# Shared experts of a two-layer MoE kernel: weights held on TensorE, the tokens' turned rows moving through

## The chip, the cores and the metric

The kernel runs on one core of a Trainium2 chip. The metric is the device time of one execution in microseconds. A core has TensorE (matmuls; PE in the views, PEld for its weight loads), VectorE (DVE), ScalarE (ACT), GpSimd (POOL) and SyncE (SP, here the issuer of most DMAs). They run their own instruction lists and wait for one another by semaphores.

## The reference, cut to what matters

Two layers over x of 8 x 256 tokens, D = 256. Each layer normalises x, computes an attention s and a mixture of experts g from the normalised rows, and adds s * silu(g) to x. The part that is changed is the shared expert of each layer, an MLP with 352 hidden columns that every token goes through:

```python
sg = silu(jnp.einsum('bsd,fd->bsf', x, Wsg))           # layer 0, FS = 352
su = jnp.einsum('bsd,fd->bsf', x, Wsu)
shared_out = jnp.einsum('bsf,df->bsd', sg * su, Wsd)
...
z = jax.nn.silu(xf @ Sg.T) * (xf @ Su.T) @ Sd.T        # layer 1, ISH = 352
```

Beside it each token goes through 2 of 8 routed experts in layer 0 and 4 of 16 in layer 1, with 176 hidden columns each. All is float32.

## The kernel before

The span begins with layer 0's attention (to about 362 us), then come layer 0's expert blocks, layer 1's attention (about 550 to 1580 us), and layer 1's expert blocks to the end. The expert part of a layer is one list of units, each of 128 rows. First come the routed units (NB0 = 39, NB1 = 79): rows gathered by expert are read from DRAM, put through that expert, and stored to DRAM (yg). Then come sixteen shared units, one for each tile of 128 tokens. I call these sixteen the shared stage of a layer, and count their tiles by c, with n = NB + c.

A shared unit goes through these helpers, which stand with the same names in pe_blocks0, act_blocks0, dve_blocks0 and in their twins for layer 1 (lines in brackets: layer 0, layer 1):

- turn_x on TensorE (L938, L1944): two transposes put the tile's rows on their side; copy_x on ScalarE (L1079, L2029) copies them to SBUF as xbT. In layer 0, from some tile on, a second pair of transposes (L942) and a small product (L950) make the logits of layer 1's router.
- shared_gate_up on TensorE (L987, L1980): xbT is the loaded (stationary) operand, the weights of gate and up move through it, 352 columns at a time: 2 projections x 2 halves of D = 4 matmuls. Gate goes to PSUM bank 2, up to bank 3, in every unit. A float32 matmul shows as two records in the trace.
- tanh on ScalarE (L1085, L2035), then the two steps of hidden on VectorE (L1147 and L1151, L2084 and L2088): silu(gate) * up, tokens on the partitions.
- turn_h on TensorE (L968, L1961): three transposes put h on its side into bank 4 or 5; copy_h on ScalarE (L1097, L2047) brings it to SBUF (the routed units copy theirs on VectorE).
- shared_down on TensorE (L996, L1989): three matmuls of 256 moving columns, to bank 6 or 7.
- combine on VectorE (L1166 and L1169; L2101 and L2106): adds the routed results of the tile's tokens, which GpSimd gathers from yg by an indirect DMA for each expert of a token, two a tile in layer 0 (L1271), four in layer 1 (L2147). Buffers for two tiles exist: the gathers for tile c start once combine(c-2) is done. The first of them waits until all routed results are stored.
- out_tanh (L1103, L2053), gate_out (L1175; L2114 and L2116), and add_out (L1180, L2121), which adds to x_res. In layer 0 the product with S, the attention's result, is made by GpSimd (mix, L1254), and VectorE then takes the statistics for layer 1's normalisation (L1188, L1190), with which GpSimd makes the reciprocal root (norm_pow, L1259 and L1261).

The order on each engine is written out by hand. TensorE, for each tile: shared_gate_up(n), logits, turn_x(n+1), shared_down(n-1) (for c = 0 the last routed unit's down instead, L976 and L978, L1969 and L1971), turn_h(n). VectorE: hidden(n), gate_out(c-2), combine(c-1), then scale, add_out and statistics of earlier tiles. GpSimd in layer 0: norm_pow(c-4), the two gathers of c, mix(c-3); in layer 1 the gathers alone. As gate and up have one pair of banks, shared_gate_up(n) waits until hidden(n-1) has read them (`pe.wait_ge(h_ready, n)`).

L1446, L1447 and L1448 are matmuls of layer 1's attention with 128 loaded and 128 (or 64) moving float32 columns.

Of the kernel before, what the change touches and what calls it, by code (L numbers as in the profile page):

```python
# [26 lines left out]
P = 128  # L27
# [82 lines left out]
def build(nc, A, out, phases=3):  # L110
    with ExitStack() as ctx:
# [177 lines left out]
        th_b = carve("blocks", 2, FS0)  # L289
# [629 lines left out]
        def pe_blocks0(pe):  # L919
# [93 lines left out]
            for c in range(TILES):  # L1013
# [9 lines left out]
                turn_h(n, FS_CHUNKS)  # L1023
# [47 lines left out]
        def act_blocks0(act):  # L1071
# [40 lines left out]
            for c in range(TILES):  # L1112
                n = NB0 + c
                tanh(n, FS0)
# [6 lines left out]
                copy_h(n)  # L1121
# [16 lines left out]
        def dve_blocks0(dve):  # L1138
            def hidden(n, width):
                routed = n < NB0  # L1140
                gate = ps[:, 2 + n % 2, 0:F0] if routed else ps[:, 2, 0:FS0]
                up = ps[:, 2 + n % 2, F0:2 * F0] if routed else ps[:, 3, 0:FS0]
                th = th_b[:, n % 2, 0:width]
# [3 lines left out]
                dve.scalar_tensor_tensor(th, th, 1.0, gate, ALU.add, ALU.mult).then_inc(half_step, 1)  # L1147
# [3 lines left out]
                dve.tensor_tensor(h_pad[:, n % 2, 0:width], th, up, ALU.mult).then_inc(h_ready, 1)  # L1151
# [51 lines left out]
            for b in range(NB0):  # L1203
                hidden(b, F0)
# [3 lines left out]
            for c in range(TILES):  # L1208
                hidden(NB0 + c, FS0)
# [710 lines left out]
        def again(sem, done):  # L1920
# [3 lines left out]
        gu4_done, th4_ready, half4_step, h4_ready, h4_turned, h4T_copied, y4_done, y4_copied = (  # L1924
            again(n, UNITS) for n in (gu_done, th_ready, half_step, h_ready, h_turned, hT_copied, y_done, y_copied))
# [7 lines left out]
        def pe_blocks1(pe):  # L1933
# [40 lines left out]
            def shared_gate_up(n):  # L1974
                pe.wait_ge(x4_copied.sem, x4_copied.at(0, n + 1))
                pe.wait_ge(h4_ready.sem, h4_ready.at(0, n))
                for which in range(2):
                    for kc in range(KC):
                        at = (2 * kc + which) * FS1
                        last = pe.matmul(ps[:, 2 + which, 0:FS1], xb4T[:, n % 2, kc * P:(kc + 1) * P], shared1[:, at:at + FS1],  # L1980
                                         start=kc == 0, stop=kc == KC - 1)
                last.then_inc(gu4_done.sem, 1)

            def shared_down(n):
                pe.wait_ge(h4T_copied.sem, h4T_copied.at(0, n + 1))
                pe.wait_ge(y4_copied.sem, y4_copied.at(0, n - 1))
                for f in range(FS_CHUNKS):
                    at = 2 * KC * FS1 + f * D
                    last = pe.matmul(ps[:, 6 + n % 2, 0:D], h4T[:, n % 2, f * P:(f + 1) * P], shared1[:, at:at + D],  # L1989
# [22 lines left out]
            for c in range(TILES):  # L2012
# [8 lines left out]
                turn_h(n, FS_CHUNKS)  # L2021
            shared_down(UNITS1 - 1)

        def act_blocks1(act):
# [6 lines left out]
            def tanh(n, width):  # L2031
                act.wait_ge(gu4_done.sem, gu4_done.at(0, n + 1))
                if n >= 2:
                    act.wait_ge(h4_ready.sem, h4_ready.at(0, n - 1))
                act.activation(th4[:, n % 2, 0:width], ps[:, 2 + (n % 2 if n < NB1 else 0), 0:width], ACT.Tanh, scale=0.5)\  # L2035
                   .then_inc(th4_ready.sem, 1)
# [6 lines left out]

            def copy_h(n):
                act.wait_ge(h4_turned.sem, h4_turned.at(0, n + 1))
                act.wait_ge(y4_done.sem, y4_done.at(0, n - 1))
                act.copy(h4T[:, n % 2, :], ps[:, 4 + n % 2, 0:HCOLS]).then_inc(h4T_copied.sem, 1)  # L2047
# [14 lines left out]
            for c in range(TILES):  # L2062
                n = NB1 + c
                tanh(n, FS1)
# [6 lines left out]
                copy_h(n)  # L2071
# [3 lines left out]
        def dve_blocks1(dve):  # L2075
            def hidden(n, width):
                routed = n < NB1
                gate = ps[:, 2 + n % 2, 0:F1] if routed else ps[:, 2, 0:FS1]
                up = ps[:, 2 + n % 2, F1:2 * F1] if routed else ps[:, 3, 0:FS1]
                th = th4[:, n % 2, 0:width]  # L2080
# [524 lines left out]
```

## Time and profile before

| | us |
|---|---|
| median of 3 runs | 1880.08 |
| lowest and highest | 1878.42, 1880.09 |
| the profiled execution's own time | 1896.83 |
| its span | 1895.0 |
| TensorE busy (PE) | 1768.4 (93%) |
| VectorE busy | 1265.7 (67%) |
| ScalarE busy | 908.8 (48%) |
| GpSimd busy | 857.2 (45%) |
| granted TensorE clock, mean over the span | 0.975 of full speed |

The span runs from the first to the last instruction of the profiled execution. A busy share is taken over the whole span, attention included; the two shared stages, from about 459 to 554 us and from about 1782 us to the end, are a tenth of it. In the views, "issue" after an arrow is time in which the engine waited for nothing that the profile shows, and "remote" a releaser that the profile doesn't know.

### The profile page before, as it was taken

To read this page: it belongs to the slowest core of one execution; us is meant where nothing else is said; L and a number is where in the kernel's file an instruction comes from. 1 tells how busy PE (TensorE), PEld (TensorE's weight loads), DVE (VectorE), ACT (ScalarE), POOL (GpSimd) and SP (SyncE) were. 2 spreads that over 40 slices of the span, in tenths; PEclk is the share of its full clock that TensorE was granted. 3 is DMA by queue.
4 is the path that set the end of the run, shared out by engine and by line. 5 is a ranking of instruction groups with operands and counts; after the bars stand their busy time and mean duration, and the time that the engine had idled before them with its cause. 6 is when DMAs were issued, how large, how long until landed. Compare 5 with 4: busy or idle time off the path is not lost.

```text
span 1895.0 us, 34165 instructions
## 1 busy us (share of the span) xinstructions
PE 1768.4 (93%) x11310; PEld 1401.9 (74%) x11310; DVE 1265.7 (67%) x2787; ACT 908.8 (48%) x2986; POOL 857.2 (45%) x943
## 2 busy tenths in 40 slices
PE   6999988899879999999999999999999997999976
PEld 4666666677658887888888888888888885777653
DVE  4888988643676888886767666666666663444465
ACT  3777767543334444444544544445445443444321
POOL 2011024100665655657767667677676661000264
PEclk8999999999989999999999999999999998999998
DMA  7965543244220000000000000000001223333333
GB/s 238 304 217 164 187 140 112 92 129 142 99 85 1 1 12 1 6 1 15 21 16 15 20 16 20 16 12 23 13 12 45 85 102 123 107 106 107 100 118 108
DMA packets 104692, 148.39 MB, mean 78 GB/s; under 512 B 11888, under 2 KB 84720, under 8 KB 102096
## 3 DMA queue, kind: packets, MB, share of 16 engines
q1 hardware_dynamic: 95168, 119.95, 19.6%
q0 software_dynamic: 9216, 25.18, 4.0%
q8 instruction: 107, 1.75, 0.4%
q10 hardware_dynamic: 144, 1.05, 0.1%
q14 instruction: 57, 0.47, 0.1%
HBM read 81.64 MB, written 64.49 MB: 77 GB/s over the span
## 4 chain that ended last, share of the span: by engine, by line
PE 78%; DVE 10%; issue 4%; POOL 3%; ACT 2%; another core or an unknown queue 1%; DMA 1%; SPq 0%; DVEq 0%; ACTq 0%; POOLq 0%
PE ps L1419 12%; PE ps L1434 9%; PE ps L1506 5%; PE ps L1952 5%; PE ps L1460 5%; PE ps L705 4%; PE ps L1448 3%; PE ps L1447 3%; PE ps L1446 3%; PE ps L959 2%; PE ps L1441 2%; PE ps L1969 2%; PE ps L1971 2%; PE ps L724 2%; PE ps L695 2%
## 5 line engine op out<-in xcount | busy, mean ns | idle before, releaser
L1419 PE MATMUL ps<-work,weights 128*128 128x256 f32 x1024 | 248.6, 386 | 1.2 <-DVE work L1692 1.1
L1434 PE MATMUL ps<-split 128*128 128x512 f32 x768 | 227.8, 419 | 0.0
L1419 PEld LDWEIGHTS ps<-work,weights 128*128 128x128 f32 x1024 | 186.3, 191 | 23.8 <-DVE work L1692 1.4
L1834 POOL TENSOR_TENSOR work<-work,rope 128x512 f32<-128x512 f32 x128 | 164.8, 1288 | 54.0 <-ACT work L1607 54.0
L2147 POOL DMA_INDIRECT work<-yg,work x64 | 62.7, 980 | 238.7 <-DMA yg<-work 207.3
L1840 POOL TENSOR_TENSOR work<-work 128x512 f32<-128x512 f32 x128 | 164.5, 1285 | 5.0
L1434 PEld LDWEIGHTS ps<-split 128*128 128x128 f32 x768 | 130.7, 190 | 24.8
L827 DVE COPY work<-ps 128x384 f32<-128x384 f32 x256 | 130.0, 549 | 19.8 <-PE ps L705 19.5
L810 ACT ACTIVATE work<-ps,work 128x128 f32<-128x128 f32 x256 | 94.5, 369 | 84.5 <-DVE work L907 74.5
L705 PE MATMUL ps<-ident,work 128*128 128x128 f32 x768 | 115.4, 282 | 17.3 <-DVE work L827 15.4
L1506 PE MATMUL ps<-weights,work 128*128 128x256 f32 x512 | 124.1, 386 | 2.5 <-ACT work L1663 2.5
L513 POOL DMA_INDIRECT xg<-work x96 | 97.2, 1013 | 62.5 <-PE ps L695 39.8
L2084 DVE SCALAR_TENSOR_TENSOR work<-work,ps 128x176 f32<-128x176 f32 (+1 forms) x95 | 35.0, 369 | 133.8 <-ACT work L2035 123.5
L1714 DVE TENSOR_TENSOR work<-ps,keep_w 128x384 f32<-128x384 f32 x128 | 65.4, 553 | 87.2 <-PE ps L1442 86.8
L812 ACT ACTIVATE work<-ps,work 128x256 f32<-128x256 f32 x256 | 121.6, 475 | 0.0
L705 PEld LDWEIGHTS ps<-ident,work 128*128 128x128 f32 x768 | 88.6, 144 | 41.7 <-ACT work L812 19.1
L1460 PE MATMUL ps<-work 64*128 64x256 f32 (+1 forms) x1024 | 106.1, 349 | 13.7 <-issue 10.9
L1648 ACT ACTIVATE work<-ps,work 128x128 f32<-128x128 f32 x256 | 90.6, 366 | 51.4 <-PE ps L1448 51.1
L1727 DVE RECIPROCAL work<-ps 128x256 f32<-128x256 f32 x64 | 111.9, 1748 | 0.0
L1506 PEld LDWEIGHTS ps<-weights,work 128*128 128x128 f32 x512 | 99.3, 194 | 17.0 <-ACT work L1663 3.1
L1613 ACT COPY work<-ps 128x256 f32<-128x256 f32 x128 | 47.2, 368 | 130.3 <-PE ps L1434 130.3
L1460 PEld LDWEIGHTS ps<-work 64*128 64x128 f32 x1024 | 86.9, 195 | 30.2 <-issue 14.1
(240 smaller groups left out, 4447.3 us busy)
## 6 DMA issues: line engine op xcount, KB each, us to landing
heads_by_part<-split SPq DMA_DIRECT2D x64, 256.0 KB, 4.1
split<-heads_by_part SPq DMA_DIRECT2D x64, 256.0 KB
work<-xg SPq DMA_DIRECT2D x118, 128.0 KB
yg<-work SPq DMA_DIRECT2D x118, 128.0 KB, 1.7
xg<-work SPq DMA_DIRECT2D x13, 1024.0 KB, 5.9
weights<-in_w SPq DMA_DIRECT2D x8, 1024.0 KB, 6.1
weights<-in_f SPq DMA_DIRECT2D x8, 1024.0 KB, 5.0
weights<-in_f SPq DMA_DIRECT2D x8, 608.0 KB, 4.4
```

The costliest lines, as they stand in the source:

```text
L513: pool.indirect_dma_start(out=rows, out_offset=bass.IndirectOffsetOnAxis(ap=self.index[:, k, c:c + 1], axis=0), in_=src, in_offset=None).t ...
L705: last = pe.transpose(ps[:, 4 + hh, k * P:(k + 1) * P], prob[:, g % RING, hh, k * P:(k + 1) * P], ident[:, :])
L812: act.activation(pr[:, P:BLK], sc[:, 0:SEQ], ACT.Exp, bias=nmax[:, g % RING, 1, hh:hh + 1], accum_out=total[:, bb, 1, h:h + 1]).then_inc(e ...
L827: dve.tensor_copy(probT[:, g % RINGT, hh, :], ps[:, 4 + hh, 0:BLK]).then_inc(probT_ready.sem, 1)
L1419: last = pe.matmul(ps[:, 2, which * SEQ:(which + 1) * SEQ], w1(h, (which * KC + kc) * P, P), xT[:, kc, :], start=kc == 0, stop=kc == KC - 1)
L1434: last = pe.matmul(ps[:, 3, :], x1_split[:, xp, kc, c * P:(c + 1) * P], w_vg[:, n % 2, wp, kc, :], start=i == 0, stop=i == KC * len(TERMS) ...
L1460: last = pe.matmul(ps[:, 4 + hh, at], k[rows, half, keys], q[rows, half, queries], start=half == 0, stop=half == 1)
L1506: last = pe.matmul(ps[:, 7, c * D:(c + 1) * D], ogT[:, hh, c * P:(c + 1) * P], weights[:, W1O + h * D:W1O + (h + 1) * D], start=h == 0 and ...
L1727: dve.reciprocal(enz[:, n % 2, :, :].rearrange("p c n -> p (c n)"), ps[:, 0, SEQ:2 * SEQ])\
L1834: pool.tensor_tensor(qk[:, h % 4, :, :], raw[:, h % 2, :, :], rope[:, 0, :].unsqueeze(1).broadcast_to([P, 2, SEQ]), ALU.mult).then_inc(rot ...
L1840: pool.tensor_tensor(qk[:, h % 4, :, :], qk[:, h % 4, :, :], rot_s[:, h % 2, :, :], ALU.add)\
L1952: last = pe.matmul(ps[:, 2 + b % 2, 0:GUW], xb4T[:, b % 2, kc * P:(kc + 1) * P], experts1[:, bass.ds(offset[b] + kc * GUW, GUW)], start=kc ...
```

## The change

The operands of the gate and up projections change places. The weights are the loaded operand, in chunks of 128, 128 and 96 of the 352 hidden columns, and xbT, 128 tokens wide, moves through. That makes 12 matmuls of 128 moving columns in place of 4 of 352. Gate and up come out with the hidden columns on the partitions, three chunks side by side in 384 columns, which is the shape that shared_down loads. So turn_h and copy_h go for shared units, and hidden's second step writes hbT itself. Gate and up get two pairs of banks, 2 and 3, 4 and 5, in turn, and shared_gate_up(n) waits for hidden of unit n-2. The last chunk's down product reads 96 rows. tanh and hidden work on 384 columns (the last chunk's rows 96 to 127 are whatever lies in the bank, and nothing reads them). The order of the rest stays.

```diff
             def shared_gate_up(n):
+
+                bank = 2 + 2 * ((n - NB0) % 2)
                 pe.wait_ge(x_copied, n + 1)
-                pe.wait_ge(h_ready, n)
+                pe.wait_ge(h_ready, max(n - 1, NB0))
+                if n == NB0 + 1:
+                    pe.wait_ge(hT_copied, NB0)
                 for which in range(2):
-                    for kc in range(KC):
-                        at = (2 * kc + which) * FS0
-                        last = pe.matmul(ps[:, 2 + which, 0:FS0], xbT[:, n % 2, kc * P:(kc + 1) * P], shared0[:, at:at + FS0],
-                                         start=kc == 0, stop=kc == KC - 1)
+                    for f in range(FS_CHUNKS):
+                        width = min(P, FS0 - f * P)
+                        for kc in range(KC):
+                            at = (2 * kc + which) * FS0 + f * P
+                            last = pe.matmul(ps[0:width, bank + which, f * P:(f + 1) * P], shared0[:, at:at + width],
+                                             xbT[:, n % 2, kc * P:(kc + 1) * P], start=kc == 0, stop=kc == KC - 1)
                 last.then_inc(gu_done, 1)
 
             def shared_down(n):
-                pe.wait_ge(hT_copied, n + 1)
+                pe.wait_ge(h_ready, n + 1)
                 pe.wait_ge(y_copied, n - 1)
                 for f in range(FS_CHUNKS):
                     at = 2 * KC * FS0 + f * D
-                    last = pe.matmul(ps[:, 6 + n % 2, 0:D], hbT[:, n % 2, f * P:(f + 1) * P], shared0[:, at:at + D],
+                    rows = min(P, FS0 - f * P)
+                    last = pe.matmul(ps[:, 6 + n % 2, 0:D], hbT[0:rows, n % 2, f * P:(f + 1) * P], shared0[0:rows, at:at + D],
                                      start=f == 0, stop=f == FS_CHUNKS - 1)
...
                     shared_down(n - 1)
-                turn_h(n, FS_CHUNKS)
...
             def tanh(n, width):
+                bank = 2 + n % 2 if n < NB0 else 2 + 2 * ((n - NB0) % 2)
                 act.wait_ge(gu_done, n + 1)
                 if n >= 2:
                     act.wait_ge(h_ready, n - 1)
-                act.activation(th_b[:, n % 2, 0:width], ps[:, 2 + (n % 2 if n < NB0 else 0), 0:width], ACT.Tanh, scale=0.5)\
-                   .then_inc(th_ready, 1)
+                act.activation(th_b[:, n % 2, 0:width], ps[:, bank, 0:width], ACT.Tanh, scale=0.5).then_inc(th_ready, 1)
...
-            def copy_h(n):
-                act.wait_ge(h_turned, n + 1)
-                act.wait_ge(y_done, n - 1)
-                act.copy(hbT[:, n % 2, :], ps[:, 4 + n % 2, 0:HCOLS]).then_inc(hT_copied, 1)
...
-                tanh(n, FS0)
+                tanh(n, HCOLS)
                 if c + 1 < TILES:
                     copy_x(n + 1)
                 if c == 0:
                     copy_y(NB0 - 1)
                 if c >= 2:
                     out_tanh(c - 2)
-                copy_h(n)
...
+            def shared_hidden(n):
+                bank, th = 2 + 2 * ((n - NB0) % 2), th_b[:, n % 2, :]
+                dve.wait_ge(th_ready, n + 1)
+                dve.scalar_tensor_tensor(th, th, 1.0, ps[:, bank, 0:HCOLS], ALU.add, ALU.mult).then_inc(half_step, 1)
+                dve.wait_ge(half_step, n + 1)
+                dve.wait_ge(y_done, n - 1)
+                dve.tensor_tensor(hbT[:, n % 2, :], th, ps[:, bank + 1, 0:HCOLS], ALU.mult).then_inc(h_ready, 1)
...
-                hidden(NB0 + c, FS0)
+                shared_hidden(NB0 + c)
...
-        h4 = carve("experts", 2, HCOLS)
+        h4 = carve("experts", 2, 2 * P)
         h4T = carve("experts", 2, HCOLS)
-        th4 = carve("experts", 2, FS1)
+        th4 = carve("experts", 2, HCOLS)
```

Layer 1 gets the same edits under its own names (h4_ready, h4T and so on). The semaphores h4_turned and h4T_copied start from NB0, where they started from NB0 + 16, as the shared units no longer count on them.

## Rows read from the trace of the kernel before

**Rows 1.** Busy by stretches: PE, PEld, DVE, ACT, POOL; clock, DMA share, GB/s.

```profile
522.01:527.38 5.37, 5.06 (x26) 3.71 (x26) 3.60 (x11) 1.86 (x5) 3.56 (x6) 1.00 0.17 50
...
1863.31:1867.89 4.58, 4.58 (x20) 2.94 (x20) 3.98 (x10) 1.57 (x4) 3.64 (x4) 1.00 0.58 171
...
1787.90:1882.00 94.10, 71.98 (x276) 47.32 (x274) 55.52 (x124) 21.82 (x57) 62.71 (x64) 0.92 0.41 121
```

**Rows 2.** The chain that ended last, layer 0: start us, us, what.

```profile
459.65 2.37 PE ps L987 x8
...
462.68 0.45 PE ps L978 x2
...
463.54 1.71 DMA yg<-work
...
467.36 6.49 DMA work<-yg,work
...
541.64 0.55 PE ps L968 x3
```

**Rows 3.** Timeline, layer 0, one period: start us, us, instruction, idle before.

```profile
522.01 0.19 POOL L1259 TENSOR_TENSOR work<-work,minus_half 128x1 f32<-128x1 f32 x1 [1.22 <-DVE work L1190]
...
526.19 0.43 DVE L1180 SCALAR_TENSOR_TENSOR x_res<-work,x_res 128x256 f32<-128x256 f32 x1 [1.63 <-POOL work L1254]
...
527.38 0.19 POOL L1259 TENSOR_TENSOR work<-work,minus_half 128x1 f32<-128x1 f32 x1 [1.22 <-DVE work L1190]
```

**Rows 4.** Who waited for whom, in 484:540 and 1787:1895 (total, times, longest).

```profile
DVE x_res L1180 <- POOL work L1254: 17.5, 10, 2.7
...
POOL work L2147 <- DVE work L2106: 12.8, 4, 4.7
```

**Rows 5.** The chain that ended last, a tile of layer 1.

```profile
1861.13 0.47 ACT work L2035
...
1861.63 0.53 DVE work L2084
...
1862.76 0.55 PE ps L1961 x3
1863.31 2.37 PE ps L1980 x8
1865.68 0.40 PE ps L1944 x2
1866.08 1.30 PE ps L1989 x6
1867.38 0.51 PE ps L1961 x3
```

**Rows 6.** Timeline, layer 1: gathers on GpSimd, VectorE's combine.

```profile
1787.90 0.99 POOL L2147 DMA_INDIRECT work<-yg,work  x1 [207.33 <-DMA yg<-work]
...
1794.22 0.95 POOL L2147 DMA_INDIRECT work<-yg,work  x1 [0.31 <-issue]
...
1794.54 0.48 DVE L2101 SCALAR_TENSOR_TENSOR work<-work,ps 128x256 f32<-128x256 f32 x1 [3.93 <-DMA work<-yg,work]
...
1887.90 0.48 DVE L2101 SCALAR_TENSOR_TENSOR work<-work,ps 128x256 f32<-128x256 f32 x1 [1.17 <-PE ps L1989]
```

**Rows 7.** ScalarE in 1782:1890 (busy, mean ns, idle before), and one tanh.

```profile
L2047 ACT COPY work<-ps 128x384 f32<-128x384 f32 x16 | 7.7, 479 | 34.9 <-remote 17.0 <-PE ps L1961 12.8 <-issue 5.1
L2035 ACT ACTIVATE work<-ps 128x352 f32<-128x352 f32 x16 | 7.4, 465 | 36.9 <-PE ps L1980 18.0 <-remote 15.2 <-issue 3.8
...
1804.20 0.47 ACT L2035 ACTIVATE work<-ps 128x352 f32<-128x352 f32 x1 [5.52 <-remote]
```

**Rows 8.** 128 by 128 matmuls of attention, their loads (ns, min/median/max).

```profile
1311.32 0.39 PE L1446 MATMUL ps<-work 128*128 128x128 f32 x2
...
1312.43 0.39 PE L1448 MATMUL ps<-work 128*128 128x128 f32 x2
...
L1448 PEld LDWEIGHTS ps<-work x512: 192/192/192, 576.5 to 1573.7; 128*128 128x128 f32 x171
```

More of the change, by code:

```diff
@@ L1138, in dve_blocks0, with hidden @@
         def dve_blocks0(dve):
[L1139 to L1143, printed above, removed]
+            def hidden(n):
+                th = th_b[:, n % 2, 0:F0]
                 if n == 0:
@@ L1203, in dve_blocks0 @@
             for b in range(NB0):
-                hidden(b, F0)
+                hidden(b)
                 if b >= 1:
@@ L1923, in build @@
         x4_turned, x4_copied = again(x_turned, UNITS + BEHIND), again(x_copied, UNITS + BEHIND)
-        gu4_done, th4_ready, half4_step, h4_ready, h4_turned, h4T_copied, y4_done, y4_copied = (
-            again(n, UNITS) for n in (gu_done, th_ready, half_step, h_ready, h_turned, hT_copied, y_done, y_copied))
+        gu4_done, th4_ready, half4_step, h4_ready, y4_done, y4_copied = (
+            again(n, UNITS) for n in (gu_done, th_ready, half_step, h_ready, y_done, y_copied))
+        h4_turned, h4T_copied = again(h_turned, NB0), again(hT_copied, NB0)
         x4_loaded = [again(xb_loaded[n], 16 * len(range(n, NB0, RINGX))) for n in range(RINGX)]
@@ L1974, in shared_gate_up @@
             def shared_gate_up(n):
+                bank = 2 + 2 * ((n - NB1) % 2)
                 pe.wait_ge(x4_copied.sem, x4_copied.at(0, n + 1))
-                pe.wait_ge(h4_ready.sem, h4_ready.at(0, n))
+                pe.wait_ge(h4_ready.sem, h4_ready.at(0, max(n - 1, NB1)))
+                if n == NB1 + 1:
+                    pe.wait_ge(h4T_copied.sem, h4T_copied.at(0, NB1))
                 for which in range(2):
[L1978 to L1981, printed above, removed]
+                    for f in range(FS_CHUNKS):
+                        width = min(P, FS1 - f * P)
+                        for kc in range(KC):
+                            at = (2 * kc + which) * FS1 + f * P
+                            last = pe.matmul(ps[0:width, bank + which, f * P:(f + 1) * P], shared1[:, at:at + width],
+                                             xb4T[:, n % 2, kc * P:(kc + 1) * P], start=kc == 0, stop=kc == KC - 1)
                 last.then_inc(gu4_done.sem, 1)
             def shared_down(n):
-                pe.wait_ge(h4T_copied.sem, h4T_copied.at(0, n + 1))
+                pe.wait_ge(h4_ready.sem, h4_ready.at(0, n + 1))
                 pe.wait_ge(y4_copied.sem, y4_copied.at(0, n - 1))
@@ L1988, in shared_down @@
                     at = 2 * KC * FS1 + f * D
-                    last = pe.matmul(ps[:, 6 + n % 2, 0:D], h4T[:, n % 2, f * P:(f + 1) * P], shared1[:, at:at + D],
+                    rows = min(P, FS1 - f * P)
+                    last = pe.matmul(ps[:, 6 + n % 2, 0:D], h4T[0:rows, n % 2, f * P:(f + 1) * P], shared1[0:rows, at:at + D],
                                      start=f == 0, stop=f == FS_CHUNKS - 1)
@@ L2063, in act_blocks1 @@
                 n = NB1 + c
-                tanh(n, FS1)
+                tanh(n, HCOLS)
                 if c + 1 < TILES:
@@ L2075, in dve_blocks1, with hidden @@
         def dve_blocks1(dve):
[L2076 to L2080, printed above, removed]
+            def hidden(n):
+                th = th4[:, n % 2, 0:F1]
                 if n == 0:
@@ L2087, in hidden, with shared_hidden @@
                     dve.wait_ge(h4_turned.sem, h4_turned.at(0, n - 1))
-                dve.tensor_tensor(h4[:, n % 2, 0:width], th, up, ALU.mult).then_inc(h4_ready.sem, 1)
+                dve.tensor_tensor(h4[:, n % 2, 0:F1], th, ps[:, 2 + n % 2, F1:2 * F1], ALU.mult).then_inc(h4_ready.sem, 1)
+            def shared_hidden(n):
+                bank, th = 2 + 2 * ((n - NB1) % 2), th4[:, n % 2, :]
+                dve.wait_ge(th4_ready.sem, th4_ready.at(0, n + 1))
+                dve.scalar_tensor_tensor(th, th, 1.0, ps[:, bank, 0:HCOLS], ALU.add, ALU.mult).then_inc(half4_step.sem, 1)
+                dve.wait_ge(half4_step.sem, half4_step.at(0, n + 1))
+                dve.wait_ge(y4_done.sem, y4_done.at(0, n - 1))
+                dve.tensor_tensor(h4T[:, n % 2, :], th, ps[:, bank + 1, 0:HCOLS], ALU.mult).then_inc(h4_ready.sem, 1)
             def copy_h(b):
@@ L2124, in dve_blocks1 @@
             for b in range(NB1):
-                hidden(b, F1)
+                hidden(b)
                 if b >= 1:
@@ L2129, in dve_blocks1 @@
             for c in range(TILES):
-                hidden(NB1 + c, FS1)
+                shared_hidden(NB1 + c)
                 if c >= 2:
```

18 lines of the change are left out of this document (6 added, 12 removed).

## The prediction

> **What bounds the kernel now.** I first read the two stages that the change touches, by the table of busy time by stretches [rows 1]. Each stage takes sixteen tiles of 128 tokens through the shared expert. In one period of layer 0's steady part TensorE is busy 5.06 of 5.37 us; over layer 1's gathers it is busy 72.0 of 94.1 us, GpSimd 62.7, VectorE 55.5. But a busy share says nothing of who waits for whom, so the next views are the chain that ended last and the timeline.
>
> Layer 0: the first projections (459.65, 2.37 us) and the down products behind them lie on the chain, up to the landing of the last routed block's y; after that it holds no TensorE instruction until 541.64. It goes through a slow landing of the first gathers (6.49 us) and then, tile after tile, through GpSimd and VectorE [rows 2]. The timeline shows this loop [rows 3]: GpSimd starts on tile c's variance at 522.01, and its next turn of the same step is at 527.38, 5.37 us later. Between lie the power, two gathers and the product with S; VectorE takes that product at 526.19, having sat idle for it for 1.63 us, adds it and takes the statistics for which GpSimd waits. Neither TensorE nor ScalarE is in the loop. In 484 to 540 us VectorE waits 17.5 us in 10 times for that product [rows 4]: whatever hidden() costs more or less goes into this idling.
>
> Layer 1: the chain through an undisturbed tile [rows 5] is tanh 0.47, two VectorE steps of 0.53, three turns 0.55, projections 2.37, with handoffs 4.58 us from tile to tile. TensorE's own work fills the same time: 2.37 + 0.40 (turn_x) + 1.30 (down) + 0.51 (turn_h) = 4.58, and the stretch shows it busy throughout [rows 1]. GpSimd has four gathers a tile. In an unbroken row each takes 0.95 us after 0.30 of issue [rows 6], 1.25 us, or 5.0 a tile: slower than 4.58, so with all engines running freely the gathers set the pace, 64 x 1.25 = 80 us. In the profiled execution they took 94.1. Of the 14 us of difference 12.8 is GpSimd waiting, 4 times, for VectorE's combine, which frees a pair of gather buffers [rows 4]. What makes VectorE late is seen at ScalarE [rows 7]: it sat idle 17.0 us before copy_h (L2047) and 15.2 before tanh (L2035) with a releaser that the view calls remote. One such wait ends at 1804.20, after 5.52 us. Layer 0's stage has none of them.
>
> **Whose time the sum is made against.** The profiled execution took 1896.83 us, the median of the runs is 1880.08: 16.75 less. Those 14 us, and a tail after the last gather that is some us longer than it need be (rival A), are about that excess. I take it as likeliest that the timed runs lack most of these waits; that they have them is a rival. So the sum is made on the profiled stages as they go where no such wait stands, and put on 1880.08.
>
> **The change part by part.**
> 1. Gate and up. Before: 4 matmuls, 8 records, of 352 moving columns, 2.37 us [rows 5]. After: 2 x 3 x 2 = 12 matmuls, 24 records, of 128 moving columns. Such matmuls, each with 128 loaded columns of its own, stand in layer 1's attention [rows 8]: twelve records of L1446 to L1448 start in pairs from 1311.32 to 1312.43, 1.11/5 = 0.222 us a pair, 0.111 each. 24 x 0.111 = 2.67 us: +0.30 a tile. One load record lasts 192 ns, more than this pace, so loads overlap the stream. Lower end: the pure rate of moving columns, 2370/(8 x 352) = 0.84 ns, x 128 x 24 = 2.59 us, +0.22. Upper end: loads do not overlap, rival B. I take 0.30, from the nearest rows.
> 2. The three turns of h go (0.51 us of TensorE), and copy_h on ScalarE. TensorE's tile of layer 1 becomes 2.67 + 0.40 + 1.30 = 4.37 us; layer 0's 5.06 - 0.51 + 0.30 = 4.85. Down's last chunk has 96 rows and the same 256 columns: nothing.
> 3. Two pairs of banks: gate_up(n) waits for h of unit n-2, not n-1. The chain of layer 1 opens: tanh and the steps of n (0.47 + 0.53 + 0.53, 1.6 with handoffs) run under gate_up(n+1), 2.67 us. Steady gain: none, as 4.58 was already under the gathers' 5.0, and 5.37 holds no TensorE. Were the gathers' cover gone, it would be worth 16 x (4.58 - 4.37) = 3.4 us in layer 1.
> 4. tanh and the two steps run over 384 columns instead of 352. Bound by proportion: 0.53 x 32/352 = 0.05 each, +0.10 us of VectorE a tile. VectorE is busy 3.98 of 4.58 us in a period of layer 1 [rows 1]; 4.1 stays under 5.0. In layer 0 it goes into the 1.63 us of idling. Cost 0; uncovered, 16 x 0.10 = 1.6 us a layer.
> 5. In TensorE's order the stage's first projections stand before down(NB-1), whose y must be copied, stored and landed before the first gather. Rows 2 show just this in layer 0: 459.65 (L987), 462.68 (L978), 463.54 (the landing). Layer 1 has the same order, and its first gather at 1787.90 waits for yg<-work [rows 6]. So the +0.30 us lies bare, once in each layer: +0.6 (at least 2 x 0.22 = 0.44).
> 6. The ends. Layer 0: on the chain TensorE comes in at 541.64 with turn_h and then the last projections. With the change they are done by then, at most 0.55 + 2.37 = 2.9 us less. But the adding behind them also waits for GpSimd's product, as in every tile [rows 4], so I take 0. Layer 1: combine(15) needs the last four gathers, 5 us after the ones before; y(15) is there by then in both kernels. 0.
> 7. The zeroing of h4 is narrower; GpSimd then waits 207 us anyway [rows 6]. shared_hidden's new wait, y_done(n-1), names a down that TensorE issues ahead of the projections just used; gate_out and combine are behind it and lose nothing. No DMA moves in any queue.
>
> Sum: +0.6 on 1880.08 = 1880.7; with the ends, 1877.6 to 1880.8; with those and the spread of the runs below, the forecast's own range is 1877 to 1882.5.
>
> **Rivals.**
> A. The timed runs have the unexplained waits as well. Then the change helps: copy_h, which met 17.0 of the 32.2 us, is gone, and a late tanh finds projections that are a tile ahead. At stake are GpSimd's 12.8 us and, at the end, combine(15) at 1887.90 [rows 6]: the last gather ends at 1882.0, and the first four, from 1787.90, ended at 1792.7 and let combine go at 1794.54, 1.9 later; so 1883.9 would do, 4.0 us. Half of 16.8 is 8.4; less 0.6 this gives 1872.3. All of it gives 1863.9. For it: the rows. Against it: the excess of 16.75, and that the waits come only beside dense gathers, which stay. It decides once over 4.4 us of the 16.8 are regained.
> B. Slower: loads do not run beside the stream. Beside gate_up TensorE has 1.7 us of work a tile in layer 1 and 5.06 - 2.37 - 0.51 = 2.2 in layer 0. So it is the bound when a record takes more than (5.0 - 1.7)/24 = 0.137 us, or (5.37 - 2.2)/24 = 0.132. At the 0.19 of a load record the periods are 6.3 and 6.8: 16 x 1.3 + 16 x 1.4 = 43 us, 1923. For it: the length of the load rows. Against it: the pace in rows 8, also where the stream is 128 columns, as here.
> The Trainium skill, TensorE: Matmul & The Clock Gate, The mechanism, has a weight load overlap matmuls in flight only where the row groups differ, which they don't here; by that rule rival B would hold, and the rows disagree with it. The section LDWEIGHTS of that page gives columns/1.2, an estimate of 107 ns for 128, which the pace of 111 is close to.
>
> **How the numbers follow.** A measurement of this kernel can tell 0.2% (3.8 us) from no change. Forecast: 0.58. A: 0.33, of which 0.29 lies beyond 3.8 us. B or a smaller form of it: 0.07. A cause not named, taken as slower: 0.02. So faster 0.29, same 0.58 + 0.04 = 0.62, slower 0.09. The range for 8 in 10 leaves out B and the rest (0.09) and the far third of A (0.11), below 1868: 1868 to 1883.
>
> **What would show it.** Right: gate_up's 24 records 0.11 us apart, 2.7 us in all; TensorE's share of the chain ending a little later before the first gather; layer 0's period again 5.37 us with VectorE waiting for GpSimd; gathers 1.25 us apart. Wrong: a pace over 0.13 us; a layer 0 stage shorter by more than 1 us, so that TensorE had a share in the loop that I did not see; or a timed gain beside shorter waits of the gathers in layer 1 (rival A).

## The result, and the profile after

| | before | after |
|---|---|---|
| median, us | 1880.08 (5 runs, 1878.42 to 1880.86) | 1866.57 (5 runs, 1863.49 to 1870.36) |
| ratio | | 0.9928, 95% interval 0.9912 to 0.9945 |
| profiled execution | 1896.83, span 1895.0 | 1866.63, span 1864.8 |

The changed kernel is 13.5 us faster. I had forecast no change, 1880.7, and a range that ended at 1868. What the change does in its own place went nearly as worked out. The chain of the changed kernel, in the columns of [rows 2]:

```profile
462.48 2.66 PE ps L993 x24
...
470.47 6.86 DMA work<-yg,work
...
1765.90 2.66 PE ps L1992 x24
```

Gate and up are 24 records in 2.66 us, in both layers. The period of layer 0, with the columns of [rows 3] and [rows 1]:

```profile
525.51 0.19 POOL L1264 TENSOR_TENSOR work<-work,minus_half 128x1 f32<-128x1 f32 x1 [1.22 <-DVE work L1195]
...
529.75 0.43 DVE L1185 SCALAR_TENSOR_TENSOR x_res<-work,x_res 128x256 f32<-128x256 f32 x1 [1.62 <-POOL work L1259]
...
530.94 0.19 POOL L1264 TENSOR_TENSOR work<-work,minus_half 128x1 f32<-128x1 f32 x1 [1.22 <-DVE work L1195]
```
```profile
525.51:530.94 5.43, 5.03 (x40) 4.63 (x39) 3.67 (x11) 1.39 (x3) 3.63 (x6) 1.00 0.17 51
...
1772.05:1855.40 83.35, 67.57 (x463) 61.88 (x461) 59.63 (x132) 17.42 (x44) 63.25 (x64) 0.93 0.47 137
```

The loop of GpSimd and VectorE takes 5.43 us where [rows 3] had 5.37, and VectorE still idles 1.62 us for GpSimd's product. From the first projections to layer 1's first attention matmul layer 0's stage took 91.2 us before and 91.3 after.

Layer 1's gathers look different: 83.35 us in place of the 94.1 of [rows 1]. ScalarE's waits there, as in [rows 7], and GpSimd's, as in [rows 4]:

```profile
L2048 ACT ACTIVATE work<-ps 128x384 f32<-128x384 f32 x16 | 7.8, 489 | 35.3 <-PE ps L1992 35.3
```
```profile
POOL work L2158 <- DVE work L2117: 2.4, 5, 0.9
```

No wait is remote, and GpSimd waits 2.4 us for buffers, not 12.8. This looks like rival A. But the comparison has a trap that I only saw later: the profiled execution of the kernel before took 1896.83 us, and none of its timed runs did. I come back to that.

The larger difference is where nothing was edited. Measured from layer 1's first attention matmul to the first shared projections of layer 1, the kernel before took 1781.9 - 550.6 = 1231.3 us and the changed one 1765.7 - 553.6 = 1212.1: 19.2 less. TensorE's code there is a loop over sequences 2 to 6 behind two unrolled ones; its last four rounds, by the table of stretches, before (two of them) and after:

```profile
1061.00:1187.30 126.30, 123.12 (x784) 104.96 (x784) 84.32 (x177) 60.21 (x176) 85.66 (x93) 0.99 0.05 18
1187.30:1312.90 125.60, 122.79 (x784) 104.97 (x784) 83.81 (x177) 60.51 (x176) 84.88 (x93) 0.99 0.04 16
```
```profile
1058.10:1179.30 121.20, 120.91 (x785) 103.56 (x785) 83.63 (x177) 60.44 (x176) 85.52 (x93) 1.00 0.05 17
1179.30:1300.40 121.10, 120.88 (x784) 103.52 (x784) 83.63 (x177) 60.34 (x175) 84.69 (x93) 1.00 0.04 15
```

The same instructions take 4.8 us more a round (125.9 against 121.1; 0.4 of it is a difference between chips, as the experiments show). One place holds nearly all of it. Of the kernel before: TensorE's waits in 935 to 1439 us, the timeline around one of them, the stretch behind it, and the page's row of the queue q8 (packets, MB, share). Then, of the changed kernel, which has no such wait, the timeline of that place and the row of q8:

```profile
PE ps L1460 <- issue: 10.9, 4, 2.9
```
```profile
1092.06 0.39 PE L1448 MATMUL ps<-work 128*128 128x128 f32 x2
1095.38 2.93 PE L1460 MATMUL ps<-work 64*128 64x256 f32 x16 [2.92 <-issue]
```
```profile
1095.38:1098.31 2.93, 2.93 (x17) 2.38 (x17) 0.00 (x0) 0.00 (x0) 0.22 (x2) 0.50 0.03 6
```
```profile
q8 instruction: 107, 1.75, 0.4%
```
```profile
1088.97 0.39 PE L1453 MATMUL ps<-work 128*128 128x128 f32 x2
1089.29 1.58 PE L1465 MATMUL ps<-work 64*128 64x256 f32 x16
```
```profile
q8 instruction: 74, 1.21, 0.3%
```

Before, TensorE stands still 2.92 us for nothing that the profile knows, and the sixteen records after that run at a granted clock of 0.50 (the lower of the two levels, 1.2 of 2.4 GHz) in 2.93 us instead of 1.58. q8 is the queue that brings instructions in packets of 16 KB. Its records of before begin at 1090.3, 1092.5, 1095.8 us and go on through the whole round, nine in each round; the changed kernel has none between 957 and 1456 us. Between two of the loop's branches the traces hold 1636 TensorE instructions. Ahead of the loop a packet of 16384 bytes begins every 255 instructions in the mean, which makes some 64 bytes for one and 256 to a packet (an estimate from these two numbers). Of the 800 instructions that the change adds 400 stand ahead of this loop, in layer 0's stage: the loop's first branch is record 13514 of TensorE before and 13914 after. They move the loop's place.

That is theory 1: the gain is the place of TensorE's loop, which is held on the chip when it touches seven packets and fetched anew in every round when it touches eight. Rival: the gain is made in the shared stages.

### The profile page after: what moved, and what is told of

It is laid out like the page before. It is cut to its first block, busy times and chain, and to the rows that moved or that the text cites. A ratio compares the mean times of both kernels' runs of the same rounds, so it can differ in the third digit from the quotient of the medians.

```text
span 1864.8 us, 34901 instructions
## 1 busy us (share of the span) xinstructions
PE 1755.5 (94%) x11726; PEld 1427.7 (77%) x11726; DVE 1263.5 (68%) x2787; ACT 895.7 (48%) x2954; POOL 856.9 (46%) x943
## 2 busy tenths in 40 slices
DMA packets 104659, 147.85 MB, mean 79 GB/s; under 512 B 11888, under 2 KB 84720, under 8 KB 102096
## 4 chain that ended last, share of the span: by engine, by line
PE 77%; DVE 10%; POOL 5%; issue 3%; DMA 3%; ACT 2%; SPq 0%; POOLq 0%; DVEq 0%; ACTq 0%
PE ps L1424 12%; PE ps L1439 9%; PE ps L1511 5%; PE ps L1958 5%; PE ps L1465 4%; PE ps L705 4%; PE ps L1452 3%; PE ps L1453 3%; PE ps L1451 3%; PE ps L959 2%; POOL work L2158 2%; DMA work<-yg,work 2%; PE ps L1446 2%; PE ps L1975 2%; PE ps L1977 2%
## 5 line engine op out<-in xcount | busy, mean ns | idle before, releaser
L1653 ACT ACTIVATE work<-ps,work 128x128 f32<-128x128 f32 x256 | 90.4, 365 | 51.7 <-PE ps L1453 51.4
L1958 PE MATMUL ps<-weights,work 128*128 x316 | 106.8, 460 | 0.2 <-ACT work L2041 0.2
L1451 PE MATMUL ps<-work 128*128 128x64 f32 (+1 forms) x512 | 97.2, 272 | 9.1 <-DVE work L1719 9.1
L1612 ACT COPY work<-ps 128x512 f32<-128x512 f32 x128 | 73.7, 576 | 65.1 <-PE ps L1424 65.1
```

Of the source, the lines that this page charges most:

```text
L1451: pe.matmul(outs[0], left[:, 0:P], rhs[0], start=True, stop=True)
L1958: last = pe.matmul(ps[:, 2 + b % 2, 0:GUW], xb4T[:, b % 2, kc * P:(kc + 1) * P], experts1[:, bass.ds(offset[b] + kc * GUW, GUW)], start=kc ...
```

## The experiments

Eighteen runs in five groups; all of a group ran on one chip, with the kernel before beside them. The groups show chips of two kinds, and this matters for every reading below. In the first, second, third and fifth group, on three chips (the third and the fifth shared one), the kernel before took 1898.39, 1899.35, 1902.29 and 1898.92 us; every trace from them has ScalarE's waits without a releaser in layer 1's shared stage (27 to 44 us of them, but for the run with half the gathers). On the fourth group's chip it took 1878.37, and no trace has any. By these signs the result was taken on a chip of the second kind (1880.08), but the trace of before that I read came from one of the first. The held rounds of the loop differ a little too: 121.5 to 121.7 us on the first kind, 121.1 on the second. No trace of a kernel with the slow loop comes from the second kind; there its price is known from times alone. So ratios are compared within a group, and stages within a kind. I call the waits late signals, for a reason shown below.

### Moving the loop, with instructions that do nothing

First group. TensorE gets repeated waits on a semaphore that is reached already (two waits make one instruction), before its first matmul:

```diff
+            for _ in range(300):        # b_c150; 128 in b_c64; a_c130: 260 in the changed kernel
+                pe.wait_ge(first_loaded, 16 * len(first_loads))
```

> The kernel before, with 300 repeated waits on a semaphore that is already reached (150 more TensorE instructions) put ahead of TensorE's first matmul, where TensorE idles anyway. Nothing of the change is in it. Theory 1 (the place of TensorE's loop): in the profiles, four rounds of TensorE's loop over sequences 2 to 6 in layer 1's attention cost 125.7 to 126.3 us each in the kernel before and 121.1 to 121.2 in the changed one, with 16 KB fetches on TensorE's instruction queue in every round of the first and none in the second; the change has 400 more TensorE instructions ahead of the loop. These 150 move the loop to a place where its 1636 instructions (64 bytes each) touch seven 16 KB blocks, as in the changed kernel, and not eight. So the periods become 121.2, the fetches go, and the time is the changed kernel's, about 1866 (1861 to 1868). Theory 2 (rival A, the gain comes from the shared stages): nothing of it is in this kernel; 1880, periods as in the kernel before.

> The same with 128 repeated waits (64 more TensorE instructions), after which the loop still touches eight 16 KB blocks. It is the control for padding as such. Theory 1: 1880, periods of about 126 us with fetches in each. Theory 2: 1880. A gain as in the kernel with 150 would mean that any displacement, or the waits themselves, bring it.

> The changed kernel, with 260 repeated waits (130 more TensorE instructions) ahead of TensorE's first matmul, after which the loop touches eight 16 KB blocks as in the kernel before. Theory 1: the four periods are 125.5 to 126.3 us again, with fetches, and the time is that of the kernel before or a little over, about 1881 (1879 to 1886). Theory 2: the shared stages keep their gain, 1866.6.

The fourth kernel is the change in layer 1 alone.

> The change in layer 1's shared experts alone; layer 0 is that of the kernel before. Its new TensorE instructions stand behind the loop, so the loop's place is that of the kernel before. Theory 1: 1880.4 (+0.3 from the first projections), periods of about 126 us with fetches. Theory 2: the gain is that of layer 1's stage, where the unexplained waits of ScalarE stood in the profile of before: 1866 to 1870, with the stage some 98.9 us long in place of 113.0.

| | time, ratio to before | the four rounds, us | q8 packets | layer 1's shared stage |
|---|---|---|---|---|
| b_c150 | 1892.54, 0.9965 [0.9951, 0.998] | 121.5 to 121.7 | 72 | 115.0 |
| b_c64 | 1919.33, 1.0102 [1.0066, 1.0137] | 129.3 to 132.0 | 107 | 115.1 |
| a_c130 | 1913.34, 1.0074 [1.0057, 1.0091] | 124.1 to 126.1 | 111 | 123.1 |
| l1_only | 1906.82, 1.0033 [1.0021, 1.0046] | 125.6 to 126.1 | 109 | 121.4 |

Which kernels fetch in every round went as theory 1 said, in all four. My times did not hold. The waits put off TensorE's first matmul, where I had taken its idle time as cover: it starts at 9.63 us without them, at 12.24 with 64 instructions, 19.34 with 130 and 21.42 with 150. In b_c64 the loop costs more than at its old place as well, as TensorE stands still twice a round. And layer 1's stage got longer with the change in it, 121 to 123 us against 115. The first matmul of b_c150, and TensorE's waits in the loop of b_c64:

```profile
21.42 1.94 PE L251 MATMUL ps<-ident,work 128*128 128x128 f32 x8 [21.42 <-issue]
```
```profile
PE ps L1460 <- issue: 17.5, 8, 2.7
```

Second group, with the padding where TensorE has idle time, at the end of each tile of layer 0's shared stage:

```diff
                 else:
                     shared_down(n - 1)
+                for _ in range(12):         # b_t96: 96 instructions; a_t128: 16 waits a tile, 128
+                    pe.wait_ge(x_copied, 1)
```

> The changed kernel once more, beside the others of this group. Theory 1 (the place of TensorE's loop) gives it 17.4 to 19.3 us less in the four rounds of the loop. Layer 1's shared stage is open: where ScalarE has no waits without a known releaser it should take 99 us, and the whole 0.9925 of the kernel before; where it has them, it took 121 to 123 us with the change in it and 113 to 115 without (runs l1_only, a_c130, b_c150, b_c64), which would leave 17.4 - 8 = 9 us, less some 3 us by which the attention of layer 0 was longer, 6 us in all, 0.997. Rival: the gain is there in the shared stages whatever the loop does, 0.993 with a stage shorter than in the next kernel by 13 us.

> The kernel before, with twelve repeated waits (six TensorE instructions) at the end of each of the sixteen tiles of layer 0's shared stage, 96 instructions in all, where TensorE is idle 0.3 us a tile. It moves the loop to the end of seven 16 KB blocks without the 7 to 13 us that the padding at the very start cost. Theory 1: periods of 121.2 to 121.6 us, no fetches between 955 and 1456 us, and 17.4 to 19.3 us less than the kernel before, a ratio of 0.990 to 0.991. So the old code in a good place would be as fast as the changed kernel or faster. Rival (the gain is in the shared stages): 1.000.

> The changed kernel with sixteen repeated waits (eight TensorE instructions) at the end of each of the sixteen tiles of layer 0's shared stage, 128 in all. TensorE has 0.5 us a tile to spare there. The loop falls into eight blocks again. Theory 1: periods of 125.6 to 126.1 us, fetches in every round, 17 to 19 us more than the changed kernel. Rival: as the changed kernel.

> The change in layer 0's shared experts alone. Its 400 more TensorE instructions place the loop as in the changed kernel; layer 1's shared stage is that of the kernel before. Theory 1: 17.4 to 19.3 us less in the loop, and faster than the kernel before by 14 to 19 us, 0.990 to 0.9925, whatever layer 1's stage does. Rival (the gain is in layer 1's shared stage): 1.000.

| | time, ratio to before | the four rounds, us | q8 packets | layer 1's shared stage |
|---|---|---|---|---|
| a_again (the changed kernel) | 1890.45, 0.9957 [0.9941, 0.9974] | 121.5 to 121.7 | 74 | 117.5 |
| b_t96 | 1881.73, 0.9908 [0.9885, 0.9931] | 121.5 to 121.7 | 72 | 113.5 |
| a_t128 | 1906.61, 1.0043 [1.002, 1.0066] | 126.0 to 126.2 | 111 | 123.1 |
| l0_only | 1884.48, 0.9922 [0.9893, 0.9952] | 121.5 to 121.7 | 73 | 112.1 |

This settles it for chips of the first kind. The old code with 96 idle instructions is 17.6 us faster than without (1899.35 - 1881.73), and faster than the changed kernel by 8.7; the changed kernel with its loop moved away is slower than the old one. On this kind of chip the change by itself costs 7 to 9 us (1890.45 - 1881.73; 1906.61 - 1899.35; in the first group 1906.82 - 1898.39), and most of it comes with layer 1's half: layer 0's alone leaves 2.8 over b_t96.

### What the change costs in layer 1's stage

Three candidates: the number of TensorE's instructions beside the gathers (theory 3), the run-ahead by two pairs of banks (theory 4), and whether the gathers are needed for it at all. Third group; b12 is b_t96 with this edit in layer 1:

```diff
-                    for kc in range(KC):
-                        at = (2 * kc + which) * FS1
-                        last = pe.matmul(ps[:, 2 + which, 0:FS1], xb4T[:, n % 2, kc * P:(kc + 1) * P], shared1[:, at:at + FS1],
+                    for f in range(FS_CHUNKS):
+                        width = min(P, FS1 - f * P)
+                        for kc in range(KC):
+                            at = (2 * kc + which) * FS1 + f * P
+                            last = pe.matmul(ps[:, 2 + which, f * P:f * P + width], xb4T[:, n % 2, kc * P:(kc + 1) * P],
+                                             shared1[:, at:at + width], start=kc == 0, stop=kc == KC - 1)
```

a_1bank has `bank = 2` in layer 1's three helpers and waits for h_ready(n) again; a_g2 has `for k in range(2)` around the gathers, so it leaves out two of a token's four routed results, and the adding reads the other two twice.

> The kernel before with its loop well placed (96 TensorE instructions in layer 0's shared stage), once more, as the reference of this group. Loop periods 121.2 to 121.7 us. Layer 1's shared stage: 112 to 115 us if this chip shows ScalarE's waits without a known releaser. If it shows none, the stage of the old code has no measurement yet: from 1880.08 less what the profile gives for the rest, about 96 us.

> The same, with layer 1's shared gate and up cut into twelve matmuls of 128, 128 and 96 moving columns, rows still loaded, in place of four of 352. Everything else of layer 1 is the old code. Theory 3 (more TensorE instructions beside the gathers make TensorE's signals come later, whatever they compute): stage 117 to 123 us where the waits exist, 4 to 9 more than the reference. Theory 4 (the run-ahead by the second pair of banks makes the waits longer): 112 to 115, as the reference. Where the waits don't exist, 0 to 1 more in both.

> The changed kernel with one pair of banks for gate and up in layer 1's shared units: the projections of a unit wait again for hidden of the unit before, and banks 2 and 3 serve all. Theory 3: stage 117 to 123 us where the waits exist, as with two pairs. Theory 4: 112 to 115. Where the waits don't exist, 99 to 101 (the changed kernel's is 99.0), as the chain of a tile is 4.2 us and the gathers are 5.0.

> The changed kernel with two of the four gathers of a tile in layer 1's shared stage; the results of two of the four routed experts of a token are left out, the adding reads the first two twice. Theory 3 and 4 both take the gathers as what the waits need: with half of them the waits without a known releaser go or fall under 5 us in sum, and the stage is bounded by TensorE's 4.37 us a tile: 6 to the first gather, 16 x 4.37 = 70 and some 6 at the end, 80 to 85 us. If the waits stay (20 us or more of them), the gathers are not what makes them.

| | time, ratio to before | layer 1's stage | late signals | GpSimd waits for VectorE |
|---|---|---|---|---|
| b_t96_2 | 1881.61, 0.9891 [0.9874, 0.9907] | 110.5 | 28.2 | 13.0 |
| b12 | 1890.81, 0.9939 [0.9922, 0.9955] | 124.1 | 41.7 | 28.7 |
| a_1bank | 1888.47, 0.9926 [0.9909, 0.9942] | 121.2 | 43.6 | 26.9 |
| a_g2 | 1856.1, one run | 80.3 | 0 | 28.3 |

ScalarE's groups in that stage, of b12, a_1bank and a_g2 (busy, mean ns, idle before):

```profile
L2039 ACT ACTIVATE work<-ps 128x352 f32<-128x352 f32 x16 | 7.4, 464 | 54.3 <-remote 29.6 <-PE ps L1984 24.5
```
```profile
L2048 ACT ACTIVATE work<-ps 128x384 f32<-128x384 f32 x16 | 7.9, 491 | 87.5 <-remote 41.7 <-PE ps L1992 37.4 <-issue 8.4
```
```profile
L2048 ACT ACTIVATE work<-ps 128x384 f32<-128x384 f32 x16 | 7.9, 491 | 48.1 <-PE ps L1992 45.7 <-issue 2.4
```

Cutting the old products into twelve, with the operands as they were, costs what the change costs: 9.2 us in time (1890.81 - 1881.61). With one pair of banks the stage stays at 121.2 us, where theory 4 had 112 to 115. Without half of the gathers the late signals are gone in the one trace, and the stage falls to the 80 us that TensorE's tile gives. So theory 4 falls, the gathers are needed, and b12 speaks for theory 3; it doesn't tell the number of TensorE's matmuls from the number of weight loads, which grew together.

What the waits are, the timeline of a_again shows:

```profile
1776.49 2.93 PE L1992 MATMUL ps<-work 128*128 128x128 f32 x24
...
1779.10 0.42 ACT L2060 ACTIVATE work<-work 128x256 f32<-128x256 f32 x1 [2.67 <-DVE work L2117]
...
1793.02 0.49 ACT L2048 ACTIVATE work<-ps 128x384 f32<-128x384 f32 x1 [13.50 <-remote]
...
1793.83 1.43 PE L1992 MATMUL ps<-work 128*128 128x128 f32 x5 [12.08 <-ACT work L2041]
```

TensorE's last record of gate_up starts at 1779.1, tanh of the same unit at 1793.02. The trace's list of semaphore events has the count for which this tanh waits rise at 1793.00; in the changed kernel's own trace it rises 0.3 us after each last record. So TensorE's signal came 13.9 us after that record began (or its last matmul ended so late: ends are modelled in this profile). The signals of the transposes and of the down product that TensorE began next, at 1779.25 and 1780.18, rise at 1793.04 and 1793.12: three signals were held up and came together. TensorE meanwhile waited for ScalarE's copy_x, queued behind that tanh, and GpSimd ran out of free buffers.

The same traces hold fewer landing records. A gather lands in sixteen parts; the buffers' two semaphores have 768 and 763 such records in the changed kernel's trace and 359 and 384 in a_again's, at the same number of DMA packets (104659). But a_g2 has only 831 of its 1024, and no late signal, so lost records alone don't make signals late. The Trainium skill, NOTIFIC — the notification-queue block, Overflow: three behaviours, one of which stalls the engine, says that a full queue of records either loses records or stalls the producer, by its setting. A stall would fit with dense gathers and with more TensorE instructions. Whether the recording is the cause no run here shows, and it stays open.

### Where a packet begins

Theory 1 names an edge, which I had counted in the compiled list as 89 instructions after the old place. Fourth group, on the chip without late signals; the padding is that of b_t96 with other counts, and b_dm is b_t96 with eight small matmuls a tile of layer 1:

```diff
+                for j in range(8):
+                    pe.matmul(ps[:, 2 + j % 2, 384:400], xb4T[:, n % 2, 0:P], shared1[:, 0:16], start=True, stop=True)
```

> The kernel before with 88 more TensorE instructions in layer 0's shared stage (six for a tile in eight tiles, five in the other eight). Theory 1, counted in the compiled instruction list: the loop's first instruction is then the last but none of a 16 KB block (place 255 of 256), so the loop still touches eight blocks: periods of 125.6 to 126.3 us with fetches, 107 or more packets on TensorE's instruction queue. If the blocks lie otherwise than I count, or if not the number of blocks decides but some distance, this and the next run are alike.

> The same with 90 instructions: the loop begins at place 1 of the next block and touches seven. Theory 1: periods of 121.5 to 121.7 us, 72 to 74 packets, some 17 us less than with 88.

> The kernel before with five TensorE instructions more in each tile of layer 0's shared stage, 80 in all, one a tile fewer than in the run with 96. Place 247, eight blocks. Theory 1: time of the kernel before, 1.000, periods near 126 us. Rival (the waits in layer 0's stage themselves or any shift help): 0.990, as with 96.

> The kernel before with its loop well placed (96 instructions), and in layer 1's shared stage eight matmuls of 16 moving columns more for a tile, into columns of banks 2 and 3 that nothing reads: 16 more matmul records and 16 more load records a tile, as many as the change adds, with hardly any columns. Theory 3 (it is the number of TensorE's instructions beside the gathers): stage 117 to 124 us, 7 to 9 us more than with 96 alone, the waits without a known releaser 5 to 15 us more. Rival (the loads of weights, the operand order or the columns): at most 8 x 2 x 0.11 = 1.8 us a tile of TensorE's time, mostly under the gathers' 5.0 us, 1 to 4 us in the stage, without more such waits.

| | time, ratio to before | the four rounds, us | q8 packets | layer 1's stage |
|---|---|---|---|---|
| b_p88 | 1865.43, one run | 121.1 | 71 | 97.8 |
| b_p90 | 1862.5, one run | 121.1 to 121.2 | 71 | 98.2 |
| b_t80 | 1861.49, 0.9911 [0.9895, 0.9928] | 121.1 to 121.2 | 72 | 97.2 |
| b_dm | 1879.03, 1.0003 [0.9993, 1.0014] | 121.1 | 73 | 111.8 |

80 and 88 were forecast slow and are fast. The edge lies between 64 (slow) and 80 (fast), so my count of it was off by 9 to 24 instructions. b_dm could not tell what it was made for: on this chip nothing is late. It adds 1.86 us to a tile in which TensorE already works 4.58, and 14 us to the stage. My price of 1 to 4 us had put most of that under the gathers' 5.0 us, which leave 0.4; a tile now takes TensorE 6.37 us without a gap (1819.46 to 1825.83). Its timeline:

```profile
1819.46 2.61 PE L1984 MATMUL ps<-work 128*128 128x352 f32 x8
...
1824.12 1.86 PE L1980 MATMUL ps<-work 128*128 128x16 f32 x16
...
1825.83 2.61 PE L1984 MATMUL ps<-work 128*128 128x352 f32 x8
```

Fifth group, the far edge, on the changed kernel:

> The changed kernel with eight repeated waits (four TensorE instructions) at the end of each tile of layer 0's shared stage, 64 in all. In the kernel before, 64 instructions more left the loop slow and 80, 88, 90, 96 and 150 made it fast, so a block begins between 65 and 80 instructions after the old place of the loop. Counted from there, the changed kernel's loop begins 65 to 80 plus 256 less than 400, so 64 to 79 instructions into a block; with 64 more 128 to 143, and it ends inside the seventh block (7 x 256 - 1636 = 156). Theory 1: periods of 121.1 to 121.7 us, 74 fetches or so; time of the changed kernel, which is 0.993 to 0.996 of the kernel before. Rival (the loop is fast only near the beginning of a block): slow, as the next run.

> The same with six TensorE instructions a tile, 96 in all. The loop begins 160 to 175 instructions into a block and so reaches into an eighth. Theory 1: periods of 125.6 to 126.3 us, 107 or more fetches, 17 to 19 us more than with 64: 1.002 to 1.006 of the kernel before. Rival (only the distance to some other code counts, not the number of blocks): as with 64.

| | time, ratio to before | the four rounds, us | q8 packets | layer 1's stage |
|---|---|---|---|---|
| a_t64 | 1889.75, 0.9952 [0.9932, 0.9973] | 121.5 to 121.7 | 75 | 119.2 |
| a_t96 | 1898.31, 0.9995 [0.9978, 1.0011] | 128.1, then 121.5 to 121.7 | 84 | 120.2 |

TensorE's waits in the loop of a_t96 and of a_t128:

```profile
PE ps L1467 <- issue: 3.9, 1, 3.9
```
```profile
PE ps L1467 <- issue: 11.3, 4, 3.0
```

64 is fast, as forecast. With 96, a few instructions into the eighth packet, the loop was fetched once more and then held; with 128 in every round. All places together, by instructions added, less 256 or 512 where that can be: held at 80, 88, 90, 96, 144 (the changed kernel), 150 and 208; fetched in every round at 0, 16, 18 and 64; once more and then held at 240. So the window is 128 to 176 places wide, where seven packets leave 7 x 256 - 1636 = 156. Its two sides are there, but "eight packets are fetched in every round" is too simple at its edge.

## Why the prediction was wrong

**The step that failed** is the frame of the sum: "the sum is made on the profiled stages", the two shared ones, with "No DMA moves in any queue" in step 7. I counted records of TensorE only for their time. The 400 instructions that layer 0's half adds have a place as well, and code behind them, whose loop turns first at 967 us, some 400 us later, changed its pace. On the chip without late signals that place is worth 1878.37 - 1861.49 = 16.9 us (b_t80); within the first kind of chip the traces give 503.6 us for the four rounds in the kernel before and 486.2 in b_t96, 17.4 less. The result's 13.5 then leave 3.4 us that the change itself costs. That is an estimate across two chips, and the intervals of the two ratios overlap. Traces of the same kind of chip have the same sign: from layer 0's first routed projection to the end 1864.8 - 364.9 = 1499.9 us in the changed kernel, and 1495.8, 1497.1 and 1498.1 in b_t80, b_p90 and b_p88.

1. **Gate and up**: right. 24 x 0.111 = 2.67 forecast, 2.66 measured. The reason behind the pace was not the moving columns, as my lower end had it: b_dm's matmuls of 16 columns come 0.112 us apart (sixteen in 1.86, the length of the last one included), and attention's of 64 and of 128 columns do the same. The Trainium skill, TensorE: Matmul & The Clock Gate, LDWEIGHTS, gives columns/1.2 for a load, an estimate of 107 ns for 128; these paces lie just above it, whatever the moving columns.
2. **Turns and copy_h go**: they do; but TensorE is busy 5.03 us in layer 0's period where the step had 4.85, 0.18 more than worked out, and it cost nothing beside GpSimd's 5.43.
3. **Two pairs of banks**: right that they bring nothing while gathers bound. Whether they bring anything elsewhere was not seen; a_1bank at 0.9926 of before, against 0.9957 (a_again) and 0.9952 (a_t64, on the same chip as a_1bank), shows no loss without them.
4. **384 columns**: right, hidden by the 1.62 us in layer 0.
5. **First projections, +0.3 a layer**: the size is that of 2.66 against 2.37. The whole stages cost more: 91.3 us against 90.4 to 90.6 in layer 0, 99.1 against 97.2 to 98.2 in layer 1 (b_t80, b_p88, b_p90), together 1.8 to 2.7 where I had 0.6. What the rest is was not found.
6. **Ends**: right, no gain seen.
7. **Zeroing and other waits**: right for the waits; the sentence on queues missed the one that fetches instructions.

**Whose time**: right. The excess of 16.75 us belonged to the chip on which the trace was taken; on the chip without late signals the old layer 1 stage is 97 to 98 us long, where the trace that I read had 113.1, and the loop's 0.4 us a round are nearly all of the rest.

**Rival A** named the waits, and their premise is false for the result's chip. The sign that I had named for it, a gain beside shorter waits of the gathers, did appear (2.4 us for 12.8), and it was the difference between two chips. Where the waits exist the change lengthens them: it is rival A with the sign turned. That its time, 1872.3 down to 1863.9, lies around the result is luck. **Rival B** falls, with records at 0.111 us.

The version that beats both kernels is the old code with 80 to 96 idle instructions in layer 0's stage: 0.9911 of before on a chip of the result's kind, 0.9908 and 0.9891 on the others, against 0.9928 and 0.9957 for the change. On the first kind its runs lie apart from the changed kernel's (at most 1882.67, at least 1883.45); on the result's kind the two intervals overlap.

**Open**: what makes TensorE's signals late on some chips, beyond dense gathers and the number of its instructions (b12 alone tells it from the operand order, and nothing tells it from the number of weight loads); where exactly a loop stops being held; what the change costs beyond 0.6 us in the two stages; and why held rounds differ by 0.4 us between the kinds of chip.

## What to carry to other kernels

When a change adds or removes instructions ahead of a long unrolled loop, look at that engine's instruction queue in the profile before and after: packets in every round, and with them a wait for nothing followed by a half-clock stretch once a round, tell that the loop is being fetched anew. Then a comparison of two codes is fair only with their loops equally placed, and some dozens of idle instructions, put where the engine has time, may be worth as much as the rewrite or more. And hold the profiled time against the timed runs first: where they differ by 1%, ask whether they come from chips of one kind before reading the trace's waits as the timed runs' waits.

## What the runs showed of the hardware that I had not expected

- A loop of 1636 TensorE instructions costs 121.1 to 121.7 us a round when held and 124.1 to 132.0 when fetched. In the kernel before, TensorE stands still 2.6 to 2.9 us at each turn, and the sixteen records behind it take 1.35 us more at the lower clock.
- 150 idle TensorE instructions ahead of the first matmul delayed it by 11.8 us (9.63 to 21.42, 79 ns each). 96 inside layer 0's shared stage, where TensorE had 0.3 us a tile to spare, cost less than 1 us (91.9 to 92.0 us in b_t96 and b_t96_2, 91.2 in the kernel before).
- A TensorE signal can reach a waiting engine 13.9 us after its last record starts, beside gathers (a_again). ScalarE waits 13.5 to 13.7 us at the same tile in a_again, l1_only, a_t128, a_t64 and a_t96, on three chips. With half of the gathers, in one trace, it is gone.
- A float32 matmul record with its own load of 128 columns comes 0.111 to 0.112 us after the one before, with 16, 64 or 128 moving columns.
